# Two per-chunk maxima over attention scores become one VectorE operation across two PSUM banks

## The reference

```
h = layernorm(x) * (1 + ca) + sa;  x = x + ga * attention(h)     # 16 heads, 4 key groups, relative bias, softmax
h = layernorm(x) * (1 + cb) + sb;  x = x + gb * experts(h)       # 16 gated experts, routing to 4 of them
h = layernorm(x) * (1 + ca) + sa;  x = x + ga * ssm(h)           # convolution, selective scan with 16 states
h = layernorm(x) * (1 + cb) + sb;  x = x + gb * tanh(h @ w @ a1 @ a2 + bias)
```

## Time and profile before

| | |
|---|---|
| median of three runs | 2464.05 us |
| profiled execution, its own time | 2462.11 us |
| its span, first to last instruction | 2460.3 us |
| mean granted TensorE clock | 0.949 of full speed |
| busy: TensorE, VectorE, ScalarE, GpSimd | 84%, 76%, 66%, 67% of the span |
| VectorE instructions | 3195, of them 512 on L728 |

### The profile page before, as it was taken

The page is one execution under the profiler, slowest core; times in us unless marked ns, Lnnn a source line. Parts: engine busy times, 40 slices in busy tenths (PEclk is TensorE's granted clock), DMA queues, the critical chain, the costliest instruction groups (busy, mean ns, idle before and its releaser), DMA issues. The chain is left out here.

```text
span 2460.3 us, 41583 instructions
## 1 busy us (share of the span) xinstructions
PE 2078.0 (84%) x11840; PEld 969.1 (39%) x11840; DVE 1862.1 (76%) x3195; ACT 1612.7 (66%) x4159; POOL 1646.0 (67%) x1836
## 2 busy tenths in 40 slices
PE   4779998989899898989899898989899997868443
PEld 2445444444444444434444444434444443323110
DVE  2544678787887878787887878787887878778885
ACT  3656666777777767677677767677777766544442
POOL 1011249686886959696977869696977868687653
PEclk9879999999999999999999999999999999989565
DMA  7735478777968787777968877787967776445351
GB/s 137 109 63 100 79 162 140 163 145 141 167 125 177 136 163 137 159 148 148 160 129 166 142 164 139 153 147 152 158 132 163 146 160 120 122 108 151 98 149 49
DMA packets 534877, 338.81 MB, mean 138 GB/s; under 512 B 353929, under 2 KB 453177, under 8 KB 534201
## 3 DMA queue, kind: packets, MB, share of 16 engines
q1 hardware_dynamic: 534652, 336.16, 69.7%
HBM read 242.21 MB, written 26.74 MB: 109 GB/s over the span
## 5 line engine op out<-in xcount | busy, mean ns | idle before, releaser
L1344 POOL TENSOR_TENSOR work<-work,bc 128x512 f32<-128x512 f32 x512 | 653.6, 1285 | 119.2 <-PE bank L1380 92.1
L1350 DVE TENSOR_TENSOR_SCAN work<-bank,work 128x512 f32<-128x512 f32 x512 | 622.1, 1215 | 136.3 <-POOL work L1344 69.5
L1357 POOL TENSOR_TENSOR work<-work,bc 128x512 f32<-128x512 f32 x436 | 564.9, 1301 | 79.3 <-DVE work L1350 77.3
L1074 POOL TENSOR_TENSOR zh<-zh,w_bc 128x512 f32<-128x512 f32 x256 | 326.7, 1276 | 406.0 <-DVE zh L1067 399.9
L1333 ACT ACTIVATE bank<-work,neg_a 128x510 f32<-128x510 f32 x512 | 354.2, 692 | 288.6 <-DVE work L1350 281.0
L738 ACT ACTIVATE probs<-bank,nmax 128x256 f32<-128x256 f32 x1024 | 478.1, 481 | 42.7 <-DVE nmax L728 42.4
L728 DVE TENSOR_REDUCE nmax<-bank 128x2 f32<-128x512 f32 x512 | 333.5, 676 | 135.7 <-PE bank L720 135.7
L748 PEld LDWEIGHTS bank<-ident,probs 128*128 128x128 f32 x2048 | 251.7, 144 | 268.9 <-issue 161.9
L748 PE MATMUL bank<-ident,probs 128*128 128x128 f32 x2048 | 319.8, 280 | 27.4 <-ACT probs_t L756 27.2
L720 PE MATMUL bank<-ke,q_all 64*64 64x256 f32 x4096 | 288.8, 399 | 56.0 <-DVE zh L1067 34.0
L756 ACT ACTIVATE probs_t<-bank 128x512 f32<-128x512 f32 x512 | 306.1, 598 | 40.8 <-PE bank L748 25.6
(11 more groups left out here) (180 smaller groups left out, 2404.9 us busy)
## 6 DMA issues: line engine op xcount, KB each, us to landing
work<-dt_rows SPq DMA_DIRECT2D x256, 512.0 KB, 7.0
ke<-low SPq DMA_DIRECT2D x256, 256.0 KB, 4.9
w_bc<-w_rows_d SPq DMA_DIRECT2D x256, 256.0 KB, 4.7
q_all<-q_rows SPq DMA_DIRECT2D x1024, 8.0 KB
bc<-bc_rows SPq DMA_DIRECT2D x64, 256.0 KB, 8.5
x_in<-in_x SPq DMA_DIRECT2D x32, 256.0 KB, 6.0
dt_rows<-step SPq DMA_DIRECT2D x16, 512.0 KB, 2.8
dt_rows<-step SPq DMA_DIRECT2D x32, 256.0 KB, 2.3
```

Source lines behind the costliest of these rows:

```text
L1074: nc.gpsimd.tensor_tensor(zh[:, n % 3, :], zh[:, n % 3, :], w_bc[:, n % WB, :], ALU.mult).then_inc(m_p, 1)
L1344: nc.gpsimd.tensor_tensor(hb[at % HB], ring[n % RING][:, 1, :], bc[:, s, :], ALU.mult).then_inc(s_dbx, 1)
L1350: nc.vector.tensor_tensor_scan(hb[at % HB], decay_bank(p, m)[:, :], hb[at % HB], 0.0, ALU.mult, ALU.add).then_inc(s_h, 1)
L1357: nc.gpsimd.tensor_tensor(hb[at % HB], hb[at % HB], bc[:, SG + batch(m)[2], :], ALU.mult).then_inc(s_hc, 1)
```

## The change

The eight PSUM tensors of one bank each become one tensor of eight banks, of which `bank[k]` is a slice. a_max_vector is called for even n only, at the place of the even chunk, waits until the scores of both chunks are there, and takes the maxima of both banks in one tensor_reduce with four outputs for each partition. It adds 2 to a_max. The place of the odd chunk holds nothing now. The exponentials and their waits are untouched.

```
-        bank = [ctx.enter_context(nc.psum_tensor(f"bank{k}", [P, 512], F32)) for k in range(8)]
+        banks = ctx.enter_context(nc.psum_tensor("banks", [P, 8, 512], F32))
+        bank = [banks[:, k, :] for k in range(8)]
...
         def a_max_vector(dve, n):
-            c = n % CHUNKS
-            dve.wait_ge(a_s, n + 1)
-            nc.vector.tensor_reduce(nmax[:, 2 * c:2 * c + 2], score_bank(n)[:, :].rearrange("p (k t) -> p k t", k=2),
-                                    AX_X, ALU.max, negate=True).then_inc(a_max, 1)
+            c, first = n % CHUNKS, 6 if n < 2 * DOUBLE and n // 2 % 2 else 0
+            dve.wait_ge(a_s, n + 2)
+            nc.vector.tensor_reduce(nmax[:, 2 * c:2 * c + 4], banks[:, first:first + 2, :].rearrange("p r (k t) -> p (r k) t", k=2),
+                                    AX_X, ALU.max, negate=True).then_inc(a_max, 2)
...
             n = chunk_due("a_max_vector", st)
-            if n is not None:
+            if n is not None and n % 2 == 0:
                 a_max_vector(dve, n)
```

## The result

Ten runs of the changed kernel have a median of 2470.93 us, ten of the one before beside them 2460.26 us. The ratio is 1.0041, with an interval from 1.0029 to 1.0053: slower by some 10 us, with 3 us of interval to either side, where 8 were forecast (2472 us). The profiled execution took 2469.89 us with a span of 2468.1 us, 7.8 us more than before. The changed kernel has one line more ahead of the operation, so L728 is L729 here, L738 is L739, L1333 is L1334 and so on, and its banks are all called "banks".

A forecast was written before the change was run, and what follows sets the result against it. No engine is full; a ring of waits from scores through the even chunk's exponential to the next scores bounds it. 6.6 + 1.1 + 0.5 = 8.2 us slower, on 2464 gives 2472 us, range 2460 to 2483.

The forecast's parts named there:

- The ring, and the slack in it: Scores, maximum, exponential of the even chunk, L1061, L1067, next scores; the even maximum has slack, the price is what exceeds it.
- the cycles like the one at 1394 us: Middle cycles, one a pair, whose exponential follows a tanh; predicted to join the waits for the maximum, some 50 in all.
- The merged operation: VectorE's one reduce over both banks: 1.23 us taken, ends 1.20 and 1.35; exponential no earlier than 1.27 us from its start.
- The routing's cycle: Cycle that ends the routing: exponential, scan and decay move by 0.55 us, passed on to the ring, 12 x 0.55 = 6.6 us.
- The cycle before the routing's: Exponential and L1061 move by 0.42 us, but VectorE is occupied until L1067: no cost, 0.06 us to spare; uncovered 5 us.
- The third cycle after: Cycle at 1394 us: exponential 0.26 us late, TensorE without a gap after it; less 0.17 regained, 12 x 0.09 = 1.1 us.
- the gift from the cycle after the routing: Without the second maximum behind L1461, L1050 starts earlier, and one TensorE cycle can start its turns some 0.17 us earlier.
- The cycle at 1446 us: Exponential 0.46 us late, but L1061 has no idle time before it: nothing; uncovered, 12 x 0.46 = 5.5 us.
- Faster: Rival: work behind the second maximum comes earlier and reaches the scores, the routing's 0.55 us is covered; 2458.5 us, chance 0.11.
- All delays pass: Rival: each exponential that moves carries the ring with it, 1.84 us a pair, 22 us: 2486 us, chance 0.12.
- No change: Rival: later joins (root chains on GpSimd, the scan's ring of buffers) take up the 0.55 us: 2464 to 2467, chance 0.24.
- The operation isn't what it says: Rival: across two banks it costs two full ones, 1.35 us, so 2475 us; chance 0.53 together with the forecast.

## Why the prediction was right

- **The ring, and the slack in it.** Right in kind. The waits of the up matmul grew by 18 us in its weight loads (some 15 forecast) and by 12 us, partly the same idle time, in its matmuls. That the exponential waits 52 times for its maximum, where some 50 were forecast, is in part luck: the cycles like the one at 1394 us were to be among them and are there once, being short by the table's measure, and 16 of the 52 lie in the head and the last pair.
- **The merged operation** was taken at 1.23 us and took 1.21; the end at 1.35 for a second bank's own start fell away. The 0.04 us to the exponential held: 1.25 us after the start where 1.27 was taken. The wait for both chunks' scores, taken at nothing, costs 0.06 us where VectorE is idle, and the operation starts 0.07 us later still; neither reaches a cycle that pays.
- **The routing's cycle, 0.55 us a pair.** Right in size (0.54) and in path: scan, decay, copy L968, L583, next scores. The run with the two maxima side by side shows that the scan's delay is enough. That the late exponential would by itself have cost nearly as much is not in the prediction, and was not run. The step that was too large is the one that let all of it last: "So 0.55 us go on to the ring". By the profiles 0.28 us are regained two cycles on, where a chain of scans on VectorE, joined to GpSimd through L799, is late by only 0.27 us. In the kernel before the decay waits 1.31 us there for a scan, and TensorE's turn then waits 0.17 us; in the changed kernel the decay waits 1.05 us and the turn not at all.

```profile
1384.24 0.69 ACT L1333 ACTIVATE bank<-work,neg_a 128x510 f32<-128x510 f32 x1 [1.31 <-DVE work L1350]
...
1385.50 0.66 PE L748 MATMUL bank<-ident,probs 128*128 128x128 f32 x4 [0.17 <-ACT probs_t L756]
```

```profile
1387.18 0.69 ACT L1334 ACTIVATE banks<-work,neg_a 128x510 f32<-128x510 f32 x1 [1.05 <-DVE work L1351]
...
1388.44 0.66 PE L749 MATMUL banks<-ident,probs 128*128 128x128 f32 x4
```

  The medians speak for more than this 0.26 us a pair, 3 us: restoring the cycle gave 6.9 us, merging it alone cost 5.2. Their intervals, some 3 us to either side and more for the first, reach down to about 3, so the difference isn't settled.
- **The cycle before the routing's.** Right: -0.01 us. From the maximum's start L1061 moved by 0.41 us, and L1067 started in its old place.
- **The third cycle after.** Taken at 0.26 us less 0.17 regained, it is 0.22 us with nothing off, 2.6 us against 1.1. The failed step is the gift from the cycle after the routing: "one cycle on TensorE can start its turns some 0.17 us earlier". The turns do start earlier, but as the catching up told above, and they do so without any merged maximum in that cycle. With it merged alone nothing is gained, since L799 takes up the 0.6 us.
- **The cycle at 1446 us** costs nothing, as said; it is even 0.06 us shorter.
- **The sum** of 8.2 us stands against 7.8 in the profile and 10 by the ratio, and the closeness is partly luck. The middle was to give 7.7 us. By its cycles it gives 12 x (0.54 - 0.28 + 0.22) = 5.8, a give-back of 3.4 us left out and a gain of 2 us that wasn't, with opposite signs; over the 11 pairs the profile has 4.2. The 3.3 us in the last 16 cycles and behind them fill the gap. The prediction took 0.5 us for head and end together, and no run assigns those 3.3 to a cause. The pair was to take 138.3 to 138.8 us and takes 138.2, longer as forecast but by less.
- **Rivals.** *Faster* lost its mechanism in the run with the cycle after the routing alone. *All delays pass* is out: two of the four cycles have covers that held. *No change* names something real, the joins that take up a delay, but they take up half of one and nothing of the other. *The operation isn't what it says* is out too, at 1.21 us.

## What to carry to other kernels

Fusing two operations on an engine that isn't the bound can cost latency: the first consumer now waits for both halves, and whatever stood between the two is pushed behind both. Go through each place in the schedule and compare three times: when the fused result is ready, when its consumer would have been free anyway, and who waits for what stood between. Of 16 places here 14 cost nothing that could be measured and two held the loss; a fused operation needn't be used in all of them, but it has to buy something where it is.

## What was not expected of the hardware

L799 multiplies two SBUF operands of 128x512 on VectorE. In the kernel before it takes 0.69 us in the head, where GpSimd is nearly idle, and up to 1.79 us later. Whenever it started inside a GpSimd operation that had more than 0.15 us left, 38 times in that kernel and 50 times in the changed one, it ended 0.55 us after the end of that operation. In all 13 traces, 595 cases, the figure lies between 0.536 and 0.554. L1389, which also reads two SBUF tensors, does the same: 0.75 us alone in four cases, and in the other 28 it ends 0.55 us after GpSimd's operation. L1050 of the same size, which takes one of its two tensors from PSUM, took 0.66 to 0.69 us in all 256 cases, 167 of which started inside a GpSimd operation. So what L799 takes beyond 0.69 us in these traces goes with GpSimd's end, not with its own work. Its mean is no measure of the kernel's speed either: it is 1001 ns before, 1091 in the changed kernel and from 936 to 1176 in the others. The Trainium skill (SBUF — State Buffer, "Who interferes with whom") states such a rule, that an instruction of VectorE with two SBUF inputs contends with GpSimd's reads of SBUF; the trace agrees, with 0.55 us as the figure. In the cycle after the routing's it made the VectorE time saved ahead of such an instruction worthless. It was read from traces; a run with L799's operand elsewhere wasn't made.

A reduction over two neighbouring banks shows no start of its own for the second in its duration: 1209 ns against 676 for one, 533 ns for 512 more elements. Two of the single ones in a row overlap by 0.08 us, so that one removed gives back about 0.05 us of VectorE (1.26 us for the pair, 1.21 for the merged one), not the 0.14 us that twice 676 ns suggests.
